# One continuous order of all batches instead of iterations with meetings, and routing weights applied to each down projection, in a two-layer attention and mixture-of-experts kernel

## What is computed

```python
x = x + attention0(layernorm(x), ctx)        # x: 8 x 256 x 128, ctx: 8 x 1601 x 128; 16 heads of 8
x = x + experts0(layernorm(x))               # 9 experts of width 352, top 2 of sigmoid scores
x = x + attention1(layernorm(x), ctx, idx)   # each query sees 64 keys, drawn with repeats from ctx rows 0..255
x = x + experts1(layernorm(x))               # 8 experts of width 176, top 2 of a softmax, and one shared expert
# an expert layer: for e: out += cw[:, e:e+1] * ((silu(x @ w1[e].T) * (x @ w3[e].T)) @ w2[e].T)
```

## Time and profile before

| | us |
|---|---|
| median of 3 runs | 1861.14 (1859.19 to 1866.93) |
| the profiled execution's own time | 1863.21 |
| its span | 1861.5 |
| mean granted TensorE clock | 0.937 of full speed |

### The profile page before, as it was taken

One profiled execution on the slowest core, in us unless ns is written; L12 is line 12 of the kernel. 1 busy time (PEld: TensorE's weight loads), 2 busy tenths in 40 slices (PEclk: granted clock), 3 DMA queues, 4 the chain that ended last, 5 costly groups with the idle time before them and its releaser, 6 DMA issues.

```text
span 1861.5 us, 34997 instructions
## 1 busy us (share of the span) xinstructions
PE 1488.8 (80%) x13168; PEld 851.4 (46%) x13168; DVE 1194.4 (64%) x2460; ACT 896.3 (48%) x2074; POOL 726.9 (39%) x1135
## 2 busy tenths in 40 slices
PE   4178788888987888887988788888888879788966
PEld 3123463336633574335733465335743357334834
DVE  4177367557876578656776578665786567765734
ACT  4157326562366524663266633665246722665231
POOL 3235215632266223652156331662236521563051
PEclk8689889898999999998999999999999989999987
DMA  7410140003200040002300041000400022000000
GB/s 212 75 28 2 37 61 19 1 2 75 44 1 2 23 74 23 2 1 50 52 19 2 7 73 39 1 2 27 70 6 1 2 53 44 2 2 8 10 1 4
DMA packets 49754, 53.69 MB, mean 29 GB/s; under 512 B 5802, under 2 KB 38964, under 8 KB 49588
## 3 DMA queue, kind: packets, MB, share of 16 engines
q1 hardware_dynamic: 49588, 51.45, 14.0%
HBM read 38.98 MB, written 12.46 MB: 28 GB/s over the span
## 4 chain that ended last, share of the span: by engine, by line
PE 38%; DMA 26%; DVE 12%; ACT 10%; POOL 6%; issue 5%; SPq 2%; ACTq 0%; POOLq 0%; another core or an unknown queue 0%; DVEq 0%
DMA k_parts<-big 16%; DMA kst<-k_parts 7%; PE ob L663 7%; PE b L649 6%; ACT probs L942 5%; DVE mx L1117 5%; PE a L635 4%; PE b L555 3%; DMA k1st<-k_parts 3%; DVE mx L1139 2%; POOL big L1388 2%; ACT big L948 2%; PE ob L504 2%; PE b L685 2%; PE a L791 2%
## 5 line engine op out<-in xcount | busy, mean ns | idle before, releaser
L1117 DVE TENSOR_REDUCE mx<-a 128x2 f32<-128x802 f32 (+1 forms) x512 | 489.3, 986 | 278.0 <-PE a L635 275.6
L942 ACT ACTIVATE probs<-b 128x512 f32<-128x512 f32 (+1 forms) x896 | 459.0, 564 | 151.8 <-PE b L649 135.9
L663 PE MATMUL ob<-probs,vaug 128*9 128x256 f32 (+1 forms) x3328 | 284.1, 392 | 3.6 <-ACT oT L884 3.6
L1371 POOL TENSOR_TENSOR big<-iotab,idx_lo 128x512 bf16<-128x512 bf16 x256 | 274.1, 1093 | 7.7
L987 ACT ACTIVATE big<-a 128x256 f32<-128x256 f32 (+2 forms) x304 | 116.1, 382 | 324.3 <-PE a L792 321.5
L649 PE MATMUL b<-big,kst 64*128 64x256 bf16 (+1 forms) x1664 | 173.5, 278 | 106.9 <-ACT big L948 48.0
L635 PE MATMUL a<-kst,qa 64*128 64x401 bf16 (+1 forms) x1024 | 175.6, 344 | 78.2 <-SPq L474 33.7
L1234 DVE SCALAR_TENSOR_TENSOR big<-big,a 128x256 f32<-128x256 f32 (+2 forms) x304 | 127.1, 418 | 128.0 <-ACT big L987 126.2
L1352 POOL CAST qst<-nm 128x4 bf16<-128x4 f32 x64 | 15.6, 244 | 409.8 <-DVE nm L1104 409.0
L1319 POOL TENSOR_TENSOR rstd<-veps,neg_half 128x2 f32<-128x2 f32 x32 | 22.6, 705 | 367.8 <-DVE veps L1035 367.7
L649 PEld LDWEIGHTS b<-big,kst 64*128 64x128 bf16 (+1 forms) x1664 | 63.2, 95 | 220.4 <-ACT probs L942 107.9
(11 more groups left out here) (262 smaller groups left out, 2435.1 us busy)
## 6 DMA issues: line engine op xcount, KB each, us to landing
kst<-k_parts SPq DMA_DIRECT2D x96, 200.1 KB
k_parts<-big SPq DMA_DIRECT2D x24, 400.2 KB, 14.5
ctx_sb<-in_ctx SPq DMA_DIRECT2D x8, 768.0 KB
k1st<-k_parts SPq DMA_DIRECT2D x96, 32.0 KB
k_parts<-kpart SPq DMA_DIRECT2D x24, 64.0 KB, 1.6
kst<-in_L_ffn_w SPq DMA_DIRECT2D x1, 1408.0 KB
x<-in_x SPq DMA_DIRECT2D x8, 128.0 KB, 2.2
out<-x SPq DMA_DIRECT2D x8, 128.0 KB, 8.0
```

The lines of the kernel that those rows point to most:

```text
L663: m = pe.matmul(ob[q:q + V1, 0:NQ], vaug[0:kn, c, 2 * p + hh, :], probs[0:kn, (2 * g + hh) % NPS, (c % 2) * NQ:(c % 2 + 1) * NQ], start=(j ...
L942: act.activation(probs[0:kn, (2 * n + hh) % NPS, 0:w], bs[(e + hh) % 3][0:kn, 0:w], ACT.Exp).then_inc(f_read, 1)
L1117: dve.tensor_reduce(mx[:, p % 2, s, :, j], bank[:, :].rearrange("p (h k) -> p h k", h=2)[:, :, 0:w], AX, ALU.max, negate=True).then_inc(m_ ...
L1371: m = pool.tensor_tensor(onehot[:, own % 2, q:q + QG, :], iotab[:, :].unsqueeze(1).to_broadcast([P, QG, P]), idx_lo[:, QG * n:QG * (n + 1) ...
```

## The change

There are no iterations and no meetings. A table (`order`) gives each piece of work of each batch a time in steps, all batches are sorted into one list `EV`, and every engine walks through the same list and does its share, in order. Batch b's attention 0 is at steps 0 to 55 of its own 56; what follows for it (`chain`, 56 later) runs mixed with the next batch's attention 0: first expert layer at steps 8 to 26, attention 1 at 34 to 49, second expert layer at 54 to 63, which is 0 to 7 of the batch after that. What precedes it (`prep`, 56 earlier: context, keys, values, queries) lies in the previous batch's steps. Twelve parts stand ahead of a batch's first step.

Routing weights are no longer spread by a matmul: the chunks are cut at the experts' borders (27 and 14), each expert has its own down projection (`dn`, L642) into a half of a0, and VectorE adds it to x with the weight as a scalar per row (L1028). PSUM is dealt out anew: gate and up take the two banks of a1; a part or `pair1` takes both banks of a0 (`m_bank`); every `dn` and 13 small transposes and projections per batch take one of them. b0 to b2 and ob stay as they were, and take the keys, values and context too. Keys go out in pieces of 512 with two copies in DRAM, and come back in four quarters (`rel`), each when the scores of its two pairs are done. x and the output share three buffers: the load of batch b waits for the store of batch b-3.

```diff
-    k_parts = nc.dram_tensor("k_parts", [3, P, NK], bf16, kind="Internal").ap()
+    k_parts = nc.dram_tensor("k_parts", [2, 3, P, NK], bf16, kind="Internal").ap()
...
         a0, a1 = psum("a0", 1024), psum("a1", 1024)
-        quarter = [a0[:, 0:512], a0[:, 512:1024], a1[:, 0:512], a1[:, 512:1024]]
-        gu_bank = quarter[0:3]
-        cb_bank = bs[0:2]
-        max_bank = [a0, a1]
-        side_bank = [bs[2][:, :], quarter[3]]
+        m_bank = [a0[:, 0:512], a0[:, 512:1024]]
+        gu_bank = [a1[:, 0:512], a1[:, 512:1024]]
+        quarter = m_bank + gu_bank
...
-        def meet(eng, k):
-            eng.drain().then_inc(met, 1)
-            eng.wait_ge(go[k], 1)
-            eng.sem_clear(go[k])
...
-        FILLS = {"s0": 2, "s1": 2, "ctx": 1, "q0": 1, "c0": 1, "cnt": 1, "q1": 1, "w1": 1, "c1": 1, "all1": 1, "cwT1": 1}
-        SLOTS = ("part", "pair1", "xT2", "pq1", "aT1", "o1", "xT3", "gate1")
...
+        M_NEED = {"part": 2, "pair1": 2, "xT4": 1, "pq0": 1, "mq": 1, "aT0": 1, "o0": 1, "xT1": 1, "gate0": 1, "xT2": 1, "pq1": 1,
+                  "aT1": 1, "o1": 1, "xT3": 1, "gate1": 1, "dn": 1}
...
+            for b in range(NB):
+                own, prep, chain = NGB * b, NGB * (b - 1), NGB * (b + 1)
...
+                for n in range(4):
+                    put(prep + 10 + 4.5 * n, "ctx", b, n)
+                    put(prep + 12.4 + 4.5 * n, "key", b, n)
+                    put(prep + 46.2 + 1.2 * n, "val", b, n)
+                for c in range(NP // 2):
+                    put(max(prep + 33, prep + 14 * c + 15), "rel", b, c)
+                for d, kind in ((35.4, "n4"), (36.9, "n4a"), (37.9, "xT4"), (45.6, "pq0"), (50.6, "lat"), (51.0, "idx")):
+                    put(prep + d, kind, b)
+                for n in range(2):
+                    put(prep + 49.6 + 0.6 * n, "all0", b, n)
+                for k in range(NH0):
+                    put(own - 5.2 + 0.42 * k if k < 12 else own + 0.82 * (k - 12) + 0.1, "part", b, k)
                 for p in range(NP):
+                    put(own + NG * p - (0.8 if p == 0 else 4.2), "q0", b, p)
+                for g in range(NGB):
+                    put(own + g, "s0", b, g)
+                    put(own + g + 2.3, "w0", b, g)
+                for p in range(NP):
+                    put(own + NG * (p + 1) + O_AT + 0.4, "ev0", b, p)
+                    put(own + NG * (p + 1) + C_AT + 0.2, "c0", b, p)
...
+                for n in range(NCNT):
+                    put(own + 3 * n + 4.1, "eq", b, n)
+                    put(own + 3 * n + 5.6, "cnt", b, n)
...
+                for d, kind in ((3.0, "nm0"), (3.6, "aT0"), (4.5, "o0"), (4.6, "n1"), (5.6, "n1a"), (6.2, "xT1"), (7.0, "gate0"), (8.0, "le0"), (8.6, "rt0"),
+                                (10.0, "msk"), (12.0, "mq"), (28.0, "n2"), (28.9, "n2a"), (29.4, "xT2"), (30.1, "pq1")):
+                    put(chain + d, kind, b)
+                for u in range(len(chunk0)):
+                    put(chain + 8.0 + u / 1.5, "gu", b, u)
+                    put(chain + 8.8 + u / 1.5, "hd", b, u)
+                for e in range(NE):
+                    put(chain + 8.8 + (J0 * e + 2) / 1.5 + 0.5, "dn", b, e)
...
+                for p in range(NP):
+                    for d, kind in ((0, "pair1"), (1.9, "q1"), (2.7, "s1"), (3.2, "mu"), (5.0, "w1"), (5.9, "c1")):
+                        put(chain + 33.8 + 1.3 * p + d, kind, b, p)
+                for d, kind in ((49.4, "nm1"), (50.3, "aT1"), (51.0, "o1"), (51.1, "n3"), (52.1, "n3a"), (52.7, "xT3"), (53.4, "gate1"), (54.2, "le1"), (54.8, "rt1")):
+                    put(chain + d, kind, b)
+                for v in range(len(chunk1)):
+                    put(chain + 53.6 + v / 1.5, "gu", b, len(chunk0) + v)
+                    put(chain + 54.4 + v / 1.5, "hd", b, len(chunk0) + v)
+                for e in range(NE):
+                    v = chunk1.index((1, e, 0))
+                    put(chain + 54.4 + v / 1.5 + 0.5, "dn", b, NE + e)
+                put(chain + 54.4 + (len(chunk1) - 1) / 1.5 + 0.6, "out", b)
+            at.sort(key=lambda v: (v[0], v[1]))
+            return [(kind, b, n) for _, _, kind, b, n in at]
...
+        for ev in EV:
+            kind = ev[0]
...
+            if kind in M_NEED:
+                slot[ev] = nslot
+                use = (0, 1) if M_NEED[kind] == 2 else (0,) if bank_used[0] < bank_used[1] else (1,)
+                m_at[ev], m_free[ev] = use[0], max(bank_used[k] for k in use) + 1
+                for k in use:
+                    bank_used[k] = nslot
+                nslot += 1
...
+                elif kind == "rel":
...
+                    if b >= 1:
+                        sp.wait_ge(f_psum, fill["s0", b - 1, NG * (2 * n + 2) - 1] + 2)
+                    for term in range(NT):
+                        src = k_parts[b % 2, KPART[term]].rearrange("(a h d) k -> h d a k", h=2, d=HD)
+                        for hh in range(2):
+                            r = SLOT * hh + HD * term
+                            sp.dma_start(kst[r:r + HD, 2 * n:2 * n + 2, 0:NK], src[hh, :, 2 * n:2 * n + 2, :]).then_inc(kst_in[n], 16)
...
-                def free_slot(m):
-                    if m >= 2:
-                        pe.wait_ge(m_read, m - 1)
-                    return max_bank[m % 2]
...
+            def free_slot(ev):
+                if m_free[ev] > 0:
+                    pe.wait_ge(m_read, m_free[ev])
+                return m_bank[m_at[ev]]
+            def max_part(b, k):
+                u, j = divmod(k, NM)
...
+                free_slot(("part", b, k))
+                n = min(KM, NK - j * KM)
+                for hh in range(2):
+                    o = SLOT * hh
+                    m = pe.matmul(m_bank[hh][:, 0:n], qa[o:o + SLOT, p, s, :], kst[o:o + SLOT, p, j * KM:j * KM + n], start=True, stop=True)
+                m.then_inc(m_psum, 1)
...
-                def gate_up(u):
...
-                    if u >= 3:
-                        pe.wait_ge(hu_done, u - 2)
-                    pe.matmul(gu_bank[u % 3][0:n, 0:NQ], wg_[l][:, c * P:c * P + n], xnT[l][:, :], start=True, stop=True)
-                    pe.matmul(gu_bank[u % 3][0:n, NQ:2 * NQ], wu_[l][:, c * P:c * P + n], xnT[l][:, :], start=True, stop=True).then_inc(gu_ready, 1)
...
-                def weights(u):
...
-                    pe.matmul(cb_bank[u % 2][0:n, 0:NQ], sel[l][:, c * P:c * P + n], cwT[l], start=True, stop=True).then_inc(cb_ready, 1)
...
-                def down(u):
...
-                    pe.wait_ge(hid_ready, u + 1)
-                    for s in range(NS):
-                        m = pe.matmul(ob[:, s * P:(s + 1) * P], hid[0:n, u % 4, s * P:(s + 1) * P], wd_[l][0:n, c, :],
-                                      start=(c == 0 and s == 0), stop=(c == (NC0, NC1)[l] - 1), skip_group_check=True)
...
+            def gate_up(b, u):
...
+                own = NCH * b + u
...
+                if own >= 2:
+                    pe.wait_ge(hid_ready, own - 1)
...
+                g = gu_bank[own % 2]
+                wa, wb = ([w[:, e * I0 + j * P:e * I0 + j * P + n] for w in (w1T, w3T)] if l == 0 else [w[:, e, 0:n] for w in (wg_sb, wu_sb)])
+                pe.matmul(g[0:n, 0:NQ], wa, xnT[l][:, :], start=True, stop=True)
+                pe.matmul(g[0:n, NQ:2 * NQ], wb, xnT[l][:, :], start=True, stop=True).then_inc(gu_ready, 1)
...
+            def down(b, e):
+                l, own = divmod(e, NE)
+                bank = free_slot(("dn", b, e))
+                pieces = down_pieces(l, own)
+                pe.wait_ge(hid_ready, NCH * b + max(u for u, _, _, _ in pieces) + 1)
+                w = (w2T, wd_sb)[l]
+                for s in range(NS):
+                    for k, (u, r0, r1, at) in enumerate(pieces):
+                        m = pe.matmul(bank[:, s * P:(s + 1) * P], hid[r0:r1, (NCH * b + u) % NHID, s * P:(s + 1) * P], w[r0:r1, at, :],
+                                      start=(k == 0), stop=(k == len(pieces) - 1))
+                m.then_inc(m_psum, 1)
...
-                def hidden(u):
...
-                    dve.wait_ge(cb_ready, u + 1)
-                    if u >= 4:
-                        dve.wait_ge(down_done, u - 3)
-                    dve.tensor_tensor(hid[0:n, u % 4, :], hu[0:n, u % 3, :], cb_bank[u % 2][0:n, 0:NQ], ALU.mult).then_inc(hid_ready, 1)
...
+                elif kind == "hd":
+                    own, nr = NCH * b + n, chunk_rows(n)
+                    g, t = gu_bank[own % 2], th[0:nr, own % NTH, :]
+                    dve.wait_ge(th_ready, own + 1)
+                    dve.scalar_tensor_tensor(out=t, in0=t, scalar=1.0, in1=g[0:nr, 0:NQ], op0=ALU.add, op1=ALU.mult).then_inc(gt_done, 1)
+                    dve.wait_ge(gt_done, own + 1)
+                    dve.tensor_tensor(hid[0:nr, own % NHID, :], t, g[0:nr, NQ:2 * NQ], ALU.mult).then_inc(hid_ready, 1)
+                elif kind == "dn":
+                    l, e = divmod(n, NE)
+                    dve.wait_ge(acc_done, accs) if accs else None
```

(3 more changed lines are left out.)

1575 lines of the change are left out of this document (651 added, 924 removed).

## The result

The changed kernel takes **2344 us** (median of 4 runs, 2335 to 2356) against 1864 us of before on the same chip: ratio 1.257, 95% interval 1.249 to 1.265. The forecast was 1890 us, range 1720 to 1990. The direction is right, the size is not: 480 us slower instead of 29.

The account below looks back on a forecast made before the run. TensorE's order of work with its waits was taken as the bound. Chain on a0 160.7, delays 31 and steps 42 to 50 27 gave a period of 219 us; 357+7x219 = 1890 us, range 1720 to 1990.

Parts of the forecast that it names:

- What bound the kernel before: Whole period of 215.3 us: TensorE's order of work, with its waits, sets the time; attention is made of hand-overs.
- Removed: Per period: weights' matmuls 10.8 us and keep-clock about 7 of TensorE, VectorE's product 15.7; also meetings and key-reload wait.
- Added: Three more expert chunks per batch, 4 us of TensorE; 36 VectorE accumulations at 0.3 to 0.35 each, 12 us.
- Two pairs become one, 0.54 us per part: Attention 1's maximum on a0: a part costs 1.45 us instead of 0.91; over 64 parts 35 us per period.
- TensorE needs 166 us per batch: TensorE's work in the new order: 179.4-10.8-7+4 = 166 us per batch.
- 219 us: Forecast period in the new order: a0's chain 160.7, hand-over delays 31, steps 42 to 50 27.
- 75%: Sign that the forecast is right: TensorE's share over a period is near 75%.
- rival 1: Overlap wins: TensorE keeps its 84% share, period 166/0.84 = 198 us, total 1743; chance 0.38 in its whole breadth.
- Over all I take 0.3: Mean delay at each of 103 hand-overs on a0, bounded by 0 and 0.47 us; 31 us per period.
- steps 42 to 50: No part is due and a0's chain stands still while scores wait for exponentials; 8.8 steps at 3.1 = 27 us.
- rival 3: Worse coupling: 0.47 us per hand-over, period 236, 2010 us; or routing on the chain, 229, 1960. Chance 0.14 with Rival 4.
- Rival 4: Late context: its load waits behind an earlier batch's store, 15 to 50 us on top; chance 0.14 with rival 3.

Follow-up runs that it names:

- e5: Kernel before without its routing weights: their matmuls and VectorE's product with them left out; 1824 us, ratio 0.979.
- e12: Kernel before with each part's reduction cut from 2 x 401 to 2 x 8 columns; 1825 us, ratio 0.980.
- e13: Kernel before without its keep-clock matmuls, 22 per period; 1873 us, ratio 1.010.
- e6: Changed kernel with VectorE's accumulation of the down projections cut from 128 to 4 columns; 2335 us, ratio 1.253.
- e3: Kernel before with one pair of banks for everything that rotated over two, order unchanged; 2152 us, ratio 1.155.
- e7: Changed kernel with each part's reduction cut from 2 x 401 to 2 x 8 columns; 1993 us, ratio 1.070.
- e10: Changed kernel with VectorE's part reductions and hidden products cut to 8 columns (parts 2 x 8) and down accumulations to 4; 1901 us, ratio 1.022.
- e16: Changed kernel with parts moved by up to three events to stand next to scores, nothing left out; 2423 us, ratio 1.301.
- e17: Changed kernel with parts moved next to scores and VectorE's part reductions, hidden products and accumulations cut short; 1866 us, ratio 1.0002.
- e2: Changed kernel with two extra unread 256-column matmuls ahead of each part, pair1 and most downs, 146 per batch; 2332 us, ratio 1.251.
- e4: Changed kernel without attention 1's maximum: its 128 matmuls and 64 reductions per batch replaced by a constant; 1796 us, ratio 0.965.
- e14: Changed kernel with two unread matmuls ahead of the first 20 parts, second-layer downs and pair1 only, 54 per batch; 2308 us, ratio 1.231.

## Why the prediction was wrong

**What bound the kernel before:** right. Attention was made of hand-overs and TensorE's order set the time; e5 and e12, which take work from TensorE and VectorE in one stage or the other, gain only 2% each.

**Removed:** wrong in sign for the keep-clock matmuls (e13) and more than twice too large for the weights (e5: 3.5 to 5 us per period of 10.8). The meetings and the key reload are gone from the path, DMA 26% to 1%, as foreseen.

**Added:** right; the accumulations took 0.346 us each (0.3 to 0.35 forecast) and cutting them short gives nothing that can be measured (e6). Missing are the 16 more entries of downs whose pieces no longer fill 128 rows.

**Two pairs become one, 0.54 us per part:** the wait is real, but the agreement of e3 in the old order, 37 us per period for 35, is in part luck: 15 are waits and 22 longer busy time of TensorE, which the forecast did not have. In the 1.45 us the reduce is 1.00 and the hand-over behind it 0.06, not 0.96 and 0.10; the sum stays. The rule of the Trainium skill that the forecast weighed (Perfetto Trace Analysis, section Matmuls: rotate groups through different PSUM banks so that a read lies under the next matmuls) is borne out by this pair of runs.

**TensorE needs 166 us per batch: this is the step that failed.** It subtracted busy times from a period of before and took the overlap of the rest, its changes of rows and its clock as fixed. Measured are 225 us. The forecast's 219 us leave 219-166 = 53 us in which TensorE is idle; measured are 281-225 = 56. So the waits came out in size as forecast, and the 62 us that are missing are nearly all TensorE's own busy time: its share came out at 80%, not near the 75% that the forecast named as its sign. The split below is over the last four periods of each run; the last column is an estimate that divides the busy time at half clock by 2.93/1.60, as the twelve entries of a down scale:

| us per period | period | TensorE busy | of it at half clock | idle | busy, all at full clock (estimate) |
|---|---|---|---|---|---|
| before | 216 | 180 | 11 | 36 | 175 |
| e3, before with one pair | 253 | 203 | 58 | 51 | 176 |
| changed | 281 | 225 | 87 | 56 | 186 |
| e7, parts read short | 234 | 208 | 51 | 26 | 185 |
| e10, all reads short | 221 | 198 | 27 | 24 | 185 |
| e16, parts next to scores | 296 | 239 | 118 | 57 | 185 |

The last column hardly moves with the waits: one pair leaves it where it was, and the mixed order has 185 with many waits or few. So the 59 us of busy time over the forecast are some 20 of the mixed order itself and some 40 of the clock. Of the 20, (231-129) x 0.094 = 9.6 may be changes of rows (e17 agrees, see above), 16 x 0.11 to 0.21 = 2 to 3 the additional entries of downs, and 2 the second layer's neighbours of 48 rows; the rest, some 6, no run explains. e10 shows the same directly: with VectorE nearly out of the way the periods are 217 to 224, above the 215 of before. So rival 1, whose 198 us came from this 166, could not happen.

**"Over all I take 0.3" (31 us) and steps 42 to 50 (27 us):** mis-sized with it. The whole term between uses is 115.5 us instead of 81, with the other matmuls that stand there and run at half clock included. The forecast had 4.1 us per step for steps 17 to 20 and 4.8 for steps 1 to 4 from its own walk, and set them aside as the densest; measured are 4.2 and 7.0 to 8.1, and 4.8 over steps 9 to 20, 4.3 over 42 to 52 where it took 3.1. The walk was right for steps 17 to 20; the smoothing was not.

**The granted clock is missing from the forecast.** It took before's 0.98 for a period as given. In the new order TensorE stands idle for 1 us or more 24 times per period, before 4 times, and its clock is at half for 99 us per period, before 14. The 87 busy us at half speed would be some 47 at full by the estimate above, 40 less. e2 shows 14 us of busy time for nearly half of it. It explains about half of the 12 us of the second layer's downs (1.74 us in e4, 2.38 here). What runs show of the order of cause: in e3 more waits bring the clock down with the same matmuls, in e7 and e10 shorter waits bring it back, and e13 and e14 show that the clock costs time.

**Rivals 3 and 4:** the period is longer than rival 3's 236, and not by rival 3's mechanism alone: TensorE's idle time is only 3 us over the forecast's. Of the routing's small operations no run takes any out. Rival 4 did not occur: TensorE never waits for the context's load in the trace, and the stores land in 1.8 us.

How the 61 us over the forecast's chain on a0 divide is a matter of bookkeeping, since the parts overlap. Taking VectorE's reads and products out (e10) brings 60 us back, 32 of them idle time of TensorE and 27 the clock; what e10 leaves is TensorE's row.

## What to carry to other kernels

Ask first whether the new order's own row fits on the bounding engine with every wait at zero; TensorE's busy time in one order is not what it will be when the same instructions stand between waits of 1 us, since the clock falls (180 to 203 us in e3), nor what a subtraction from another order gives (166 forecast, 184 to 190 by the estimate at the full clock in the mixed runs that keep all the matmuls). Mixing two streams hid nothing here while one pair of banks had a reader of 1 us: cutting its 64 reads short brought 47 us per period, where with two pairs it brought 4.5. Split a match between forecast and measurement into busy and idle time before calling the mechanism right; e3's 37 for 35 was 15 and 22. When a hand-stepped stretch contradicts the average that one would like to take, believe the stretch.

## What the hardware showed that was not expected

- The same matmuls with more waits get a lower clock: 0.937 to 0.855 for e3. TensorE's busy time then grows by 22 us per period, more than its idle time (15).
- 22 matmuls per period whose results nobody reads save 13 us of 1861 (e13). In the changed kernel 146 of them save nothing that can be told from no change (e2), and 54, in the stretches of low clock alone, save 2% (e14).
- Between a matmul of up to 64 rows and one of more lie 0.09 us more than between two of a kind, in either direction. A 48-row float32 entry follows another after 0.21 us in the changed kernel, where 128 rows take 0.11; in the kernel before, whose 48-row chunk stands alone, 16 of 24 took 0.11, so the rows alone do not set it.
- Twelve entries of a down take 1.60 us at the upper level of the clock and 2.93 at the lower.
